# A two-pass mixture-of-experts and attention kernel: pass 1 sorted and run in four parts instead of three, region ends cleared from a stream of their own, and a new order of turns on every engine

## What is computed

```python
x = x + 0.5 * ffn(layernorm(x), Wg, bg, W1, b1, W2, b2)     # pass 0
x = x + attn(layernorm(x), Wq, Wk, Wv, Wo)
x = x + 0.5 * ffn(layernorm(x), Wg, bg, W1, b1, W2, b2)     # pass 1

def ffn(x, ...):   # D = 128, H = 512, E = 8 experts, the best K = 2 of each row
    scores = softmax(x @ Wg + bg); topk_probs, topk_idx = top_k(scores, 2)
    eo[e] = gelu(x @ W1[e] + b1[e]) @ W2[e] + b2[e]
    return sum over the two chosen of topk_probs * eo[chosen]

def attn(x, ...):  # 16 heads of 8 channels; row s attends to rows s-8 .. s of its sequence
    scores = q . k_window / 0.56; attn = softmax(scores) . v_window; return attn @ Wo
```

## Time and profile before

| | |
|---|---|
| median of 3 runs | 1034.41 us (1033.97 to 1045.52) |
| the profiled execution, its own time | 1039.25 us |
| its span in the trace | 1037.5 us, mean granted clock of TensorE 0.933 |
| busy PE, DVE, ACT, POOL | 842.0, 643.9, 500.8, 671.5 us |
| idle time of the queues' issuing engine SP, longest causes | tile loads behind PE 120.8 us, id loads behind result scatters 118.8 us, first loads behind row scatters 93.0 us |

### The profile page before, as it was taken

How to read it: one execution, slowest core, us unless ns; L and a number is a source line. 1 busy time by engine, 2 the same in 40 slices (tenths; PEclk the granted TensorE clock), 3 DMA queues, 4 the chain that set the end, 5 groups by cost and what they waited for, 6 DMA issues and landing times.

```text
span 1037.5 us, 22518 instructions
## 1 busy us (share of the span) xinstructions
PE 842.0 (81%) x6345; PEld 736.0 (71%) x6345; DVE 643.9 (62%) x1309; ACT 500.8 (48%) x1215; POOL 671.5 (65%) x593
## 2 busy tenths in 40 slices
PE   4348996899789999988999649888987959966973
PEld 3247895898578877876778536777876948955973
DVE  4876354334489988989899989688871602300232
ACT  4546753474355547557365145644335625433431
POOL 3586777668788884456786466357867667665552
PEclk9999988999989999999999879999996989997996
DMA  9414333832155211461121211422222235732873
GB/s 293 131 46 114 84 76 86 199 78 70 52 108 142 58 48 29 102 138 35 35 57 40 96 58 38 77 63 70 55 61 67 66 79 126 163 113 58 211 167 130
DMA packets 170488, 96.44 MB, mean 93 GB/s; under 512 B 137712, under 2 KB 154406, under 8 KB 169604
## 3 DMA queue, kind: packets, MB, share of 16 engines
q1 hardware_dynamic: 152420, 59.29, 24.7%
q0 software_dynamic: 17952, 35.71, 11.6%
HBM read 25.77 MB, written 52.35 MB: 75 GB/s over the span
## 4 chain that ended last, share of the span: by engine, by line
PE 26%; DVE 15%; issue 9%; DMA 7%; SPq 7%; POOL 5%; ACT 2%; ACTq 0%; DVEq 0%; POOLq 0%
PE bank L983 10%; PE bank L966 7%; POOL x_sorted L595 5%; DMA x_sorted<-hl,slots_all 3%; SPq L473 3%; PE bank L881 2%; DVE prod L1175 2%; DVE prod L1221 2%; PE bank L854 2%; PE bank L868 2%; DVE prod L1186 2%; DMA xsT<-x_sorted 2%; DVE y_sb L1440 1%; SPq L477 1%; DMA y_in<-y_pairs 1%
## 5 line engine op out<-in xcount | busy, mean ns | idle before, releaser
L609 POOL DMA_INDIRECT y_pairs<-y_sb,tile_ids x305 | 356.3, 1168 | 198.1 <-issue 150.4
L595 POOL DMA_INDIRECT x_sorted<-hl,slots_all x256 | 306.6, 1198 | 153.3 <-issue 79.5
L770 ACT ACTIVATE h_f<-bank,b_cols 128x256 f32<-128x256 f32 (+1 forms) x736 | 264.3, 438 | 283.9 <-PE bank L966 278.2
L983 PE MATMUL bank<-w_sb,h_f 128*128 x2440 | 322.5, 284 | 2.4 <-ACT h_f L770 2.3
L983 PEld LDWEIGHTS bank<-w_sb,h_f 128*128 128x128 f32 x2440 | 297.9, 197 | 8.6 <-issue 4.3
L966 PE MATMUL bank<-xsT,w_hl 128*128 128x256 f16 (+1 forms) x2208 | 253.6, 265 | 58.1 <-DMA xsT<-x_sorted 56.5
L966 PEld LDWEIGHTS bank<-xsT,w_hl 128*128 x2208 | 196.8, 102 | 92.4 <-issue 66.3
L1440 DVE TENSOR_TENSOR y_sb<-bank,tile_ids 128x256 f32<-128x256 f32 (+1 forms) x184 | 68.3, 374 | 200.0 <-PE bank L983 197.5
L1221 DVE TENSOR_TENSOR prod<-score,qkv 128x2304 f32<-128x2304 f32 x32 | 81.6, 2549 | 0.2
L1175 DVE TENSOR_TENSOR prod<-qkv 128x2304 f32<-128x2304 f32 x32 | 81.4, 2551 | 0.2
L881 PE MATMUL bank<-prod,ident 128*128 128x256 f32 x288 | 69.6, 393 | 3.3 <-DVE prod L1221 2.9
(11 more groups left out here) (159 smaller groups left out, 847.9 us busy)
## 6 DMA issues: line engine op xcount, KB each, us to landing
y_in<-y_pairs SPq DMA_DIRECT2D x28, 512.0 KB, 5.2
x_sorted<-no_rows SPq DMA_DIRECT2D x7, 720.0 KB, 4.8
y_pairs<-y_sb,tile_ids POOLq DMA_INDIRECT x305
x_sorted<-hl,slots_all POOLq DMA_INDIRECT x256
x_sorted<-no_rows SPq DMA_DIRECT2D x56, 72.0 KB, 1.6
x_sb<-in_L_attn_x SPq DMA_DIRECT2D x3, 1024.0 KB, 6.5
out<-x_sb SPq DMA_DIRECT2D x3, 1024.0 KB
xsT<-x_sorted SPq DMA_TRANSPOSE x184
```

Source lines behind the costliest of these rows:

```text
L595: pool.indirect_dma_start(out=x_sorted[p], out_offset=bass.IndirectOffsetOnAxis(ap=slots_all[:, at:at + 1], axis=0), in_=hl[:, c % 2, i // ...
L609: pool.indirect_dma_start(out=y_pairs, out_offset=bass.IndirectOffsetOnAxis(ap=tile_ids[:, t.n % IDS, i, 0:1].bitcast(U32), axis=0), in_=y ...
L770: ins = act.activation(h_part(t, b)[:, k, :], bank[h_banks.uses[u][0]][:, k * t.slots:(k + 1) * t.slots], ACT.Gelu, bias=b1_cols[:, bass.d ...
L983: ins = pe.matmul(into[:, half, :], h_part(t, c // t.per)[:, c % t.per, half * P:(half + 1) * P], w2_flat[:, bass.ds((e * HC + c) * D, D)] ...
```

## The change

`SPLITS` now gives pass 1 four parts of one group each, so there are eight parts, all with 24 tiles: 192 tiles (120 wide, 72 narrow) instead of 184 (121 and 63), 312 result scatters instead of 305, eight plans instead of seven. `LATE_BEGIN` moves to (5, 16), part 5's tile 16. `clear_tails` becomes a stream of SP's own, `tails`, with a turn (letter c) for every four of a part's eight clearings. All five order strings are new. The diff, the strings cut to their first line:

```diff
-SPLITS = (((0,), (1,), (2,), (3,)), ((0, 1), (2,), (3,)))
+SPLITS = (((0,), (1,), (2,), (3,)), ((0,), (1,), (2,), (3,)))
...
-LATE_BEGIN = (4, 24)
+LATE_BEGIN = (5, 16)
...
 SP_ORDER = (
-    "tttttttttttttttttttttttttttttyyttttyytttttttttttttttttttttttyytttyyttttttttttttttttttyyttttyytttttttttttttttyy"
+    "ccttttttcttttctttcttttttttttttttttytyyytttttttcttttttttttttttttytyyytcttttttttttttttttctttttyytttyyttttttttttc"
...
                     sp.dma_start(x_sorted[p][bass.ds(row, TAIL), :].rearrange("(p i) c -> p i c", p=P),
                                  no_rows[:].to_broadcast([P, TAIL // P, ROW // 2])).then_inc(tails_cleared[p], DMA)
+                    if e % 4 == 3:
+                        yield
...
             def tiles():
                 for t in ALL_TILES:
                     if t.at == 0:
-                        clear_tails(t.p)
                         rows_sorted(t.p)
                     load_x(t)
                     if t.at == LOADS and t.p + 1 < NP:
                         clear_spare(t.p + 1)
                     yield
+
+            def tails():
+                for p in range(NP):
+                    yield from clear_tails(p)
...
-            take_turns(SP_ORDER, t=tiles(), y=results())
+            take_turns(SP_ORDER, t=tiles(), c=tails(), y=results())
```

## The result

The change makes the kernel slower: 1053.15 us (median of 4 runs, 1051.47 to 1055.26) against 1038.48 beside it, a ratio of 1.0149 with a 95% interval of 1.0108 to 1.0189. The forecast was 1017 us and a range of 1002 to 1036, so the sign is wrong too. The profiled execution took 1051.47 us for a span of 1049.4, which is 11.9 us more span than before.

A forecast was written before the change was run, and what follows sets the result against it. DVE and PE together were taken to bound the attention groups, a chain through routing and POOL's scatter the tail. +5 (attention's end) - 6 - 16 + 0 = -17 us, applied to the median 1034.4, gave 1017 us; range 1002 to 1036.

The forecast's parts named there:

- Group 3's scatter: Tail: POOL's 32 row moves of group 3 share the queue with 42 result moves, 98 us instead of 114.
- last row to end: From POOL's last row move to the kernel's end: the last part has the same tiles, 98.5 us, change 0.
- the clearings add nothing: PE's 9.37 us of idle time goes, but in the tail it lay beside POOL's 98 us: worth 0.
- End of attention to first row move: Wait before group 3's row scatter: 50 us instead of 56, between slots after 41 to 54 and POOL's 45.
- DVE before the end: Up to attention's end: ten more results 3.0 us, one more plan 7.4, one combine step 1.4, sum +12.
- The waits credited: Attention groups: finer parts remove DVE's 6.14 us wait, and lighter PE in the fourth group gives 1 us.
- the +24: Latest slip of attention's end: 12 us of DVE plus 12 us of PE that finds no gap.
- PE's 20 us: Added PE work before attention's end, hidden in 66 us of PE idle time; kept for the upper end.
- The start: Start of attention, 248 us in the kernel before: the forecast's sum had no term for a shift.
- D: Rival: PE becomes the bound of the attention groups, attention ends 36 us later, 1048 us in all; chance 0.09.
- C: Rival: POOL enters the tail with 44 queued moves, group 3's scatter begins no earlier, 1030 us; chance 0.22.
- The closing list: What would make it wrong: SP standing at a combine's load for POOL, or DVE at pass 1's combine step.

The follow-up runs named there:

- after_head_clear: The changed kernel with all eight clearings of a part back at the head of the part, other turns as they are: 1065.86 us, ratio 1.0254.
- parts_old_turns: The changed kernel's parts, plans and clearing stream, but every engine's turns rebuilt from the kernel before by tile number: 1071.2 us, ratio 1.0331.
- after_early_clear: The changed kernel with only the clearing turns of parts 1, 2 and 3 put back to the heads of those parts: 1056.63 us, ratio 1.0189.

## Why the prediction was wrong

**Group 3's scatter, -16: right** (97.5 us measured, 98 forecast), and **last row to end, 0: right** (98.7 against 98.5). The mechanism was named rightly too: bursts with results between them, no landing waited for. That the clearings add nothing was wrong as a statement about this order: `after_head_clear` puts them at 13 us. The sum came out, since the 98 us assumed a PE that is not held up, and only with the stream is it so. The 0 behind it is right in part by luck: part 7's first tile begins 8.8 us behind the last row move (959.5 against 950.7), since PE still has narrow tiles of part 6, where before it was 4.9 us; from there to the end it is 89.9 us instead of 93.6.

**End of attention to first row move, -6: wrong, 0.** The slots came 46.6 us after the end (843.8 against 797.2), against 40.5 before. I had put 41 to 54. POOL made 42 moves in these 56 us (20 of rows and 22 of results; 42 x 1.28 = 54) where I had counted 12 and 18 to 20, which is 45 us, so it was POOL's queue that the rows stood behind, 9.4 us longer than their slots.

**DVE before the end, +12: right** (457.4 us busy against 446.2 in the earlier trace rows, +11.2). `parts_old_turns` has the plan's 7 us in the group where it was put.

**The waits credited, -7: this step failed.** It is 12.4 us of DVE idle time more (87.2 against 74.8), and 4.6 of a later start that the sum did not have. With them the end of attention slipped by 28.1 us, beyond the +24 that I had set as the upper bound. I credited one wait, the 6.14 us of the earlier trace rows, as if all behind it would move up, and 1 us for a lighter PE. The wait went, and others took its place. The other wait of the earlier trace rows, 8.21 us for row halves, I had seen, and I wrote that one of group 3's chunks is now wanted earlier; "I credit nothing for it" was the sentence that should have carried a price. The price was for the whole ring of buffers, not for that one place: in the first group these waits of DVE are as long as before (9.8 against 9.6 us). The third buffer gives it: 16.0 us in the change against 2.1 before, so 14 of the 28 (10 by the whole time). What remains, 14.2, is DVE's +12 and 2 of start, which is the sum's own term.

**PE's 20 us, charged nothing: right.** PE's doses (15.6 us more, 10.0 and 20.6 less) moved the end by 1 to 3 us, and with the third buffer the ten tiles ahead bring no idle time. As an upper bound on hidden costs it was the wrong row to keep, since the cost lay in ACT's and POOL's order of row chunks, which the forecast did not price.

**The start, 0: wrong, +4.6.** With the third buffer it is +2.0; the clearing turns were not the cause (`after_early_clear`), and what was stays open.

**The rivals.** D had the right side and came within some 5 us (1048), with 0.09, by a mechanism that the doses refute. C had one step right: POOL came to group 3's rows with a full queue (42 moves in 56 us; C counted 44), so the scatter began no earlier. The rival that was missing: a buffer filled by one engine (ACT) and emptied by another (POOL), whose turns were both moved. The closing list of what would make the forecast wrong named SP and DVE standing for POOL, not ACT. The range reached to 1036 and left D out.

The part of the Trainium skill used there ("SBUF — State Buffer", section "Who interferes with whom") changed no term. POOL's indirect moves took 98.01/72 = 1.36 us in the first attention group of the change and 73.45/74 = 0.99 in its tail, as before. The forecast found no row that shows one instruction holding another; there are such rows, and they contradict the inference (last section).

## What to carry to other kernels

When a change moves turns on several engines, list each ring of buffers whose writer and reader both moved, and price the wait at it, also for the engine that stands there with its whole queue. The quickest test of such a cost is one buffer more, with all turns unchanged: here it gave back 16 of 28 us, where lightening PE, ACT and POOL gave 0.3. Run it in the kernel before as well, since part of the gain may be the buffer's own, and look at the stages: a long wait may give nothing back and a short one much. And look for the gain's own cause: the orders of bursts and clearings gave all of it. Without the rest of the change they are 1.3% faster than the kernel before and 2.7% faster than the change (the third buffer on top of them was not run).

## What the runs showed of the hardware that was not expected

SP's loads of tiles stand 2.53 us apart at the least (239.54 and 242.07 in the timeline of the kernel before), while the PE work of a narrow tile is 1.83. In the change's tail this shows: PE begins two narrow tiles 2.53 us apart there (938.43 and 940.96), each behind a short wait for its rows; the second:

```profile
940.96 1.14 PE L972 MATMUL bank<-xsT,w_hl 128*128 128x128 f16 x12 [0.20 <-DMA xsT<-x_sorted]
```

Eight narrow tiles for four wide ones made attention begin 9.6 us later, where I would have said 2. A clearing is 1.03 us of SP (8.21 us for eight). With before's turns, clearing turns amid the loads of pass 0 made attention start 5.6 us late; with the change's turns attention starts 4.2 to 4.5 us earlier with them than without, and at the end of the kernel they gain 13 us.

A tensor_tensor of DVE on two SBUF operands holds POOL's indirect moves. In the change's first attention group 15 moves begin under one of DVE's two large products (L1181 and L1227). They take 1.60 to 3.33 us, 2.68 in the mean, and each ends 0.83 to 0.87 us after the product does; the other 58 take 1.03 in the mean. One of them, DVE's row and POOL's:

```profile
265.06 2.56 DVE L1181 TENSOR_TENSOR prod<-qkv 128x2304 f32<-128x2304 f32 x1 [0.24 <-ACT qkv L704]
...
265.14 3.33 POOL L601 DMA_INDIRECT x_sorted<-hl,slots_all  x1 [0.30 <-issue]
```
